# Second attention: the inverse softmax sums are spread over the heads' rows as a high and a low part, in two one-row-per-step passes

## The reference, cut to what matters

```python
Qp = query @ Wq + bq
K = _l2norm(key @ Wk + bk)
V = value @ Wv + bv
Q = _l2norm(Qp)
scores = jnp.einsum('bhqd,bhkd->bhqk', Q, K) * SCALE
attn = jax.nn.softmax(scores, axis=-1)
out = jnp.einsum('bhqk,bhkd->bhqd', attn, V)
...
out = out @ Wo + bo
x = out + Qp
mu = jnp.mean(x, axis=-1, keepdims=True)
var = jnp.mean((x - mu) ** 2, axis=-1, keepdims=True)
return (x - mu) / jnp.sqrt(var + LN_EPS) * ln_gamma + ln_beta
```

## Time and profile before

| | kernel before |
|---|---|
| median of three executions | 1012.98 us |
| the profiled execution | 1015.24 us |
| its span, first to last instruction | 1013.5 us |
| mean granted TensorE clock over the span | 0.948 of full speed |
| TensorE busy | 910.0 us (90%), 5517 matmuls |
| VectorE busy | 772.3 us (76%), 1837 instructions |
| ScalarE busy | 544.6 us (54%) |
| GpSimd busy | 351.3 us (35%) |
| the 42 float32 matmul instructions of the spreads in blocks 1 to 7 | first start 747.2, last start 930.2 us |

### The profile page before, as it was taken

The page is one execution under the profiler, slowest core; times in us unless marked ns, Lnnn a source line. Parts: engine busy times, 40 slices in busy tenths (PEclk is TensorE's granted clock), DMA queues, the critical chain, the costliest instruction groups (busy, mean ns, idle before and its releaser), DMA issues. The chain is left out here.

```text
span 1013.5 us, 17873 instructions
## 1 busy us (share of the span) xinstructions
PE 910.0 (90%) x5517; PEld 763.0 (75%) x5517; DVE 772.3 (76%) x1837; ACT 544.6 (54%) x1480; POOL 351.3 (35%) x409
## 2 busy tenths in 40 slices
PE   5899999999999969999899999946999999999535
PEld 4899999999999958888799999945655555555324
DVE  5698788788787567877677777757569888867977
ACT  4677567567566455444144444414465656554367
POOL 3134334334334236555600000067545465311320
PEclk9899999999999979999999999976999999999758
DMA  9999950000000023332133333351211011000003
GB/s 311 297 309 311 320 154 0 0 0 0 0 0 2 1 84 125 110 126 84 75 113 120 121 126 124 109 159 31 59 36 37 27 42 42 1 1 1 0 10 156
DMA packets 52616, 91.84 MB, mean 91 GB/s; under 512 B 5335, under 2 KB 27584, under 8 KB 52544
## 3 DMA queue, kind: packets, MB, share of 16 engines
q1 hardware_dynamic: 46400, 74.16, 23.7%
q0 software_dynamic: 6144, 16.79, 4.9%
HBM read 34.56 MB, written 56.36 MB: 90 GB/s over the span
## 5 line engine op out<-in xcount | busy, mean ns | idle before, releaser
L462 POOL TENSOR_TENSOR prob<-prob,row_inv 128x462 f32<-128x462 f32 (+1 forms) x96 | 83.8, 875 | 185.0 <-DVE row_inv L623 184.9
L794 PE MATMUL acc<-u,probT 128*128 128x256 f32 (+1 forms) x960 | 133.5, 289 | 0.9 <-DVE u L635 0.9
L522 ACT ACTIVATE prob<-score,neg_max 128x77 f32<-128x77 f32 x512 | 121.1, 350 | 13.3 <-DVE neg_max L617 13.0
L2287 POOL DMA_INDIRECT routed<-dispatched,slots x64 | 65.2, 1019 | 173.4 <-POOLq L1392 155.9
L748 PE MATMUL score<-m,xnT 128*128 128x462 f32 (+1 forms) x576 | 125.0, 355 | 0.0
L794 PEld LDWEIGHTS acc<-u,probT 128*128 128x128 f32 (+1 forms) x960 | 119.4, 189 | 1.9 <-DVE u L635 1.4
L748 PEld LDWEIGHTS score<-m,xnT 128*128 128x128 f32 x576 | 97.8, 191 | 6.3
L1098 PE MATMUL py<-w1T,hidT 128*128 x426 | 91.1, 349 | 0.4 <-DVE hidT L1316 0.4
L1367 POOL DMA_INDIRECT dispatched<-xn,slots x64 | 68.5, 1070 | 62.6 <-DVEq L1230 45.5
L512 ACT ACTIVATE probT<-tr 128x512 fp32r<-128x512 f32 (+1 forms) x96 | 51.7, 542 | 68.5 <-PE tr L734 68.1
L1843 PE MATMUL score<-qT,kbd 128*128 128x512 f32 (+1 forms) x240 | 79.4, 442 | 0.9 <-DVE qT L2068 0.7
(11 more groups left out here) (377 smaller groups left out, 2162.1 us busy)
## 6 DMA issues: line engine op xcount, KB each, us to landing
dispatched<-zeros SPq DMA_DIRECT2D x1, 33664.0 KB, 114.4
xn<-dispatched SPq DMA_DIRECT2D x71, 128.0 KB, 2.0
dispatched<-hid SPq DMA_DIRECT2D x71, 128.0 KB, 1.7
out<-x_res SPq DMA_DIRECT2D x8, 512.0 KB, 2.6
x_res<-in_x SPq DMA_DIRECT2D x1, 3072.0 KB, 15.2
consts<-in_L_ffn_W SPq DMA_DIRECT2D x8, 384.0 KB
consts<-in_L_ffn_Ws SPq DMA_DIRECT2D x3, 384.0 KB
x_res<-in_x SPq DMA_DIRECT2D x2, 512.0 KB, 9.3
```

Source lines behind the costliest of these rows:

```text
L462: gp.tensor_tensor(pr, pr, row_inv[t % 2][:, heads(k)].unsqueeze(2).to_broadcast([P, BANK_HEADS[k], KEYS]), ALU.mult).then_inc(prob_ready, 1)
L522: last = act.activation(prob[t % 2][:, h * KEYS:(h + 1) * KEYS], score_of(t, k)[:, n * KEYS:(n + 1) * KEYS], ACT.Exp, bias=neg_max[t % 2][ ...
L794: last = pe.matmul(acc[t % 2][:, 0:D], probT[t % 2][i][0:rows, c, :], u[k][0:rows, c, :], start=(c == 0 and q == 0), stop=(c == KCH - 1 an ...
L2287: gp.indirect_dma_start(out=routed[n % 2][:, k, j, :], out_offset=None, in_=xd, in_offset=bass.IndirectOffsetOnAxis(ap=g["slots"][:, n, k, ...
```

## The change

The spread is done on operands that a one-row-per-step pass can take. Once, during set-up, ScalarE rounds the 0/1 matrix into a new tile `spread_sums` of the one-pass type. In each block VectorE writes the reciprocals in place over `osum`, then copies them rounded into `oinv_hi`, then subtracts to have the rest in `oinv_lo`; each of the three steps raises `oinv_ready`, and each waits for the one before it. TensorE multiplies the high part and then the low part into the same bank. The same is done for the halves after block 7.

To make room, the last layer's small tiles now lie in the probability buffers `prob`, so that their filling moves: the bias load waits for the last value product, the two memsets move from ahead of block 0 to the end of GpSimd's list.

```diff
@@ attention1
-        oinv = sb("oinv", [P, TB], F32)
+        oinv_hi, oinv_lo = (sb(f"oinv_{n}", [P, TB], F32R) for n in ("hi", "lo"))
+        spread_sums = sb("spread_sums", [P, sum(SUM_ROWS)], F32R)
+        sum_spread = [spread_sums[:, sum(SUM_ROWS[:i]):sum(SUM_ROWS[:i + 1])] for i in range(DC + 1)]
...
-        ffn_bias, ident16 = sb("ffn_bias", [1, D], F32), sb("ffn_ident", [P, P], BF16)
+        ident16, ffn_bias = prob[0][:, 0:P // 2].bitcast(BF16), prob[2][0:1, 0:D]
...
@@ pe_spread (pe_spread_last alike)
-            pe.wait_ge(s["oinv_ready"], n + 1)
+            pe.wait_ge(s["oinv_ready"], 3 * (n + 1))
             if 3 * n + i:
                 pe.wait_ge(s["oT_ready"], 3 * n + i)
-            pe.matmul(wide[0:rows, :], g["spread_sum"][i][at, :], oinv[at, :], start=True, stop=True).then_inc(s["wide_mm"], 1)
+            pe.matmul(wide[0:rows, :], sum_spread[i][at, :], oinv_hi[at, :], start=True, stop=False)
+            pe.matmul(wide[0:rows, :], sum_spread[i][at, :], oinv_lo[at, :], start=False, stop=True).then_inc(s["wide_mm"], 1)
@@ ScalarE
+        def act_sum_spread(act):
+            act.activation(spread_sums[:, :], g["sum_spread"], ACT.Copy)
@@ VectorE
+        def dve_split_inverse(dve, m, at):
+            dve.wait_ge(s["oinv_ready"], 3 * m + 1)
+            dve.tensor_copy(oinv_hi[0:SUM_END, at], g["osum"][0:SUM_END, at]).then_inc(s["oinv_ready"], 1)
+            dve.wait_ge(s["oinv_ready"], 3 * m + 2)
+            dve.tensor_tensor(oinv_lo[0:SUM_END, at], g["osum"][0:SUM_END, at], f32(oinv_hi[0:SUM_END, at]), ALU.subtract).then_inc(s["oinv_ready"], 1)
+
         def dve_inverse_sums(dve, n):
             dve.wait_ge(s["sums_out"], 3 * (n + 1))
-            dve.reciprocal(oinv[0:SUM_END, :], g["osum"][0:SUM_END, :]).then_inc(s["oinv_ready"], 1)
+            dve.reciprocal(g["osum"][0:SUM_END, :], g["osum"][0:SUM_END, :]).then_inc(s["oinv_ready"], 1)
+            dve_split_inverse(dve, n, slice(0, TB))
@@ dve_inverse_sums_last: the same, with tokens(a) and dve_split_inverse(dve, LAST + a, tokens(a))
@@ SyncE
+                sp.wait_ge(s["pv_mm"], NC3 * (NBLK))
                 sp.dma_start(ffn_bias[:, :], w["L1_ffn_bias"].unsqueeze(0)).then_inc(fs["bias_in"], 16)
@@ GpSimd: from ahead of block 0 to behind gp_last_rstd_half(gp, 1)
+                gp.wait_ge(s["pv_mm"], NC3 * (NBLK))
                 gp.memset(bias_rows[:, :], 0.0).then_inc(fs["rows_set"], 1)
                 gp.memset(minus_one[:, :], -1.0).then_inc(fs["rows_set"], 1)
@@ ScalarE, set-up
-                for n in range(3):
+                for n in range(2):
                     act_weights(act, n)
+                act_sum_spread(act)
+                act_weights(act, 2)
```

More of the change, by code:

```diff
@@ L888, in attention1_constants @@
     at = [SUM_SPREAD_AT + sum(SUM_ROWS[:i]) for i in range(DC + 1)]
+    g["sum_spread"] = consts[:, SUM_SPREAD_AT:SUM_SPREAD_AT + sum(SUM_ROWS)]
     g["spread_sum"] = [consts[:, a:a + rows] for a, rows in zip(at, SUM_ROWS)]
@@ L1656, in attention1 @@
         SPREAD = [(b, c) for b in range(B) for c in range(C3)]
-        bias_rows, minus_one = sb("ffn_bias_rows", [BIAS_END, D], BF16), sb("ffn_minus_one", [BIAS_END, P], BF16)
-        ffn_bias, ident16 = sb("ffn_bias", [1, D], F32), sb("ffn_ident", [P, P], BF16)
+        ident16, ffn_bias = prob[0][:, 0:P // 2].bitcast(BF16), prob[2][0:1, 0:D]
+        minus_one, bias_rows = prob[1][0:BIAS_END, 0:P // 2].bitcast(BF16), prob[1][0:BIAS_END, P:P + D // 2].bitcast(BF16)
         amax, limit = sb("x_amax", [P, 1], F32), sb("x_limit", [1, 2], F32)
@@ L1826, in pe_spread_last @@
             at, rows = slice(SUM_AT[i], SUM_AT[i] + SUM_COLS[i]), SUM_ROWS[i]
-            pe.wait_ge(s["oinv_ready"], LAST + 1 + a)
+            pe.wait_ge(s["oinv_ready"], 3 * (LAST + 1 + a))
             if a == 0 and i == 0:
@@ L1831, in pe_spread_last @@
                 pe.wait_ge(s["acc_out"], 3 * LAST + i + 1)
-            pe.matmul(last_spread(i, a)[0:rows, tokens(a)], g["spread_sum"][i][at, :], oinv[at, tokens(a)], start=True, stop=True).then_inc(s["wide_mm"], 1)
+            bank = last_spread(i, a)[0:rows, tokens(a)]
+            pe.matmul(bank, sum_spread[i][at, :], oinv_hi[at, tokens(a)], start=True, stop=False)
+            pe.matmul(bank, sum_spread[i][at, :], oinv_lo[at, tokens(a)], start=False, stop=True).then_inc(s["wide_mm"], 1)
         def pe_scores(pe, n, c):
@@ L2110, in dve_inverse_sums_last @@
                 dve.wait_ge(s["sums_out"], 3 * (LAST + 1))
-            dve.reciprocal(oinv[0:SUM_END, tokens(a)], g["osum"][0:SUM_END, tokens(a)]).then_inc(s["oinv_ready"], 1)
+            dve.reciprocal(g["osum"][0:SUM_END, tokens(a)], g["osum"][0:SUM_END, tokens(a)]).then_inc(s["oinv_ready"], 1)
+            dve_split_inverse(dve, LAST + a, tokens(a))
         def dve_divide_last(dve, i, a):
@@ L2395, in _ @@
                 gp_gather(gp, 2, 2)
-                gp.memset(bias_rows[:, :], 0.0).then_inc(fs["rows_set"], 1)
-                gp.memset(minus_one[:, :], -1.0).then_inc(fs["rows_set"], 1)
                 for n in range(NBLK):
@@ L2406, in _ @@
                 step = lambda n: gp.wait_ge(fs["part_step"], n)
+                gp.wait_ge(s["pv_mm"], NC3 * (NBLK))
+                gp.memset(bias_rows[:, :], 0.0).then_inc(fs["rows_set"], 1)
+                gp.memset(minus_one[:, :], -1.0).then_inc(fs["rows_set"], 1)
                 gp.wait_ge(fs["bias_in"], 16)
```

## The result

| | kernel before | changed kernel |
|---|---|---|
| median | 1011.12 us (20 executions) | 1017.02 us (20 executions) |
| lowest | 1009.25 us | 1011.44 us |
| ratio to before, 95% interval | | 1.0049 [1.0037, 1.0061] |
| the profiled execution's span | 1013.5 us | 1015.6 us |

The time lies inside the range, but the sum said +0.8 us and "no change", and the measurement says +5.0 us (1.0049), more than the 0.3% that can be told from no change. The case with a chance of 0.20 came. One of the changed kernel's twenty executions took 1803.52 us at a granted clock of 1.00; it is left out of the ratio, and without it the median is 1016.92.

The account below looks back on a forecast made before the run. TensorE looked like the bound, VectorE close behind. Blocks 2 to 5 +1.32, block 1 -0.10, block 6 -0.06, block 7 -1.18, afterwards +0.80: +0.78 on 1012.98 gave 1013.8 us, range 1009.0 to 1017.5.

Parts of the forecast that it names:

- The case with a chance of 0.20: Whole kernel: slower than before by over 0.3%, chance 0.20.
- What bounds the kernel: Inner blocks: TensorE looks like the bound, with VectorE arriving nearly together at the `proj` hand-over and the second transposes.
- TensorE's gain: Spreads on TensorE: two passes take 0.59 us instead of 1.02, saving 0.43 a spread, 1.28 a block.
- VectorE's cost: Between reciprocals and `qp`: a cast of 0.43 and a subtraction of 0.69 bring `qp` 1.18 us later.
- The dear ends: Rival: copy at 0.69 us gives 1015.9, with bare second weight loads too 1017.0; chance 0.14.
- Blocks 2 to 5: Each block loses 1.08 us at the hand-over and wins 0.75: +0.33 each, +1.32 in all.
- 0.10 of slack: Hand-over of `proj`, blocks 2 to 6: 0.1 us of slack cuts the 1.18 us delay to 1.08.
- blocks 1 and 6: Block 1: 1.18 lost, 1.28 won, -0.10 us; block 6: 1.08 lost, 1.14 won, -0.06 us.
- Block 7: No query projection there: first spread 0.10 us late, the 1.28 of the spreads won, -1.18 us.
- The clock: Rival: new standstills of 1.08 and 0.53 us lower the clock in blocks 1 to 6, giving 1024 us; chance 0.08.
- After block 7: Casts and subtractions for both halves add 1.5 us ahead of the first division; the last division ends +0.80 us later.
- At nothing: Set-up copy, moved memsets and bias load lie in idle time or far ahead of use: 0 us.

Follow-up runs that it names:

- e2: Changed kernel with TensorE's part only: no cast or subtraction, both passes multiply the rounded reciprocals; timed -8.9 us against the kernel before.
- e3: Changed kernel with VectorE's part only: cast and subtraction stay, spreads are float32 products of the unsplit reciprocals; timed +8.5 us against the kernel before.
- e11: e4 with float32 spreads after block 7, last-norm statistics moved between the query splits, their aggregation behind the second; timed -0.7 us against the kernel before.
- e14: Kernel before with only the last-norm statistics moved between the query splits and their aggregation behind the second; timed +3.3 us against the kernel before.
- e7: e3 with one useless subtraction of 256 columns added in block 7 between cast and subtraction; timed +11.8 us against the kernel before.
- e1: Changed kernel with the small step `shift_f` moved ahead of the reciprocals on VectorE; timed +4.3 us against the kernel before.
- e4: Changed kernel with VectorE's order reciprocals, `shift_f`, first `qp`, then cast and subtraction; ratio 0.9979 to the kernel before.

## Why the prediction was right or wrong

**What bounds the kernel: right.** TensorE and VectorE arrive nearly together at the hand-over of `proj` and at the second transposes. e2 and e3 move an inner block by -0.83 and +1.25 us, so both are on the path. That ScalarE, and the path to `y`, would come next (e11, e14) the prediction did not say; nothing in its sum hangs on it.

**TensorE's gain: right, a little large.** A pair takes 0.64 us and not 0.59, so a spread saves 0.38, not 0.43. The second load lies under the first product (920.86 and 920.94 are the starts of two loads of 0.15 and 0.16 us, the products start 0.31 apart), so the rule of the Trainium skill ("TensorE: Matmul & The Clock Gate", Part 3, section "The mechanism"), by which it would be bare, does not show here (the same section also lets a load into the background weight buffer go ahead, which no run here can tell apart).

**VectorE's cost: right.** 0.42 and 0.69 against 0.43 and 0.69; `qp` 1.18 later as worked out. The slope behind it was part luck: it set a subtraction of 512 columns beside a copy of 256 out of PSUM (0.415), and the subtraction of 256 columns then took 0.42 as well. The dear ends of that rival did not come.

**Blocks 2 to 5: the mechanism was right, the size too small**, +0.42 each and not +0.33. I took 0.10 of slack off the stall and so let all that follows be 1.08 late. But the slack was TensorE's. VectorE runs nearly without a break from the reciprocals to its first division (0.14 us of idle time before), so its own list passes on the full 1.18, and a little more (+1.25 in e3). The other side, 0.75 won, measured 0.83 in e2. In blocks 1 and 6 the same 0.1 to 0.2 is missing.

**Block 7: the step that failed.** It said "with 1.18 and a signal it is 0.10 late, and the rest is won", -1.18, and it looked only at the spread, the one consumer of what was split. But what stands behind an inserted step on its engine is delayed as well, and `shift_f` stood there. Its path over ScalarE's norm, the exponentials and the score bank had 0.3 us of slack in the kernel before (exponentials at 923.34, scores at 924.37, where after they follow within 0.72), and the split took 1.2. The wait gave the gain back (parts: +0.86 and -0.86), and the lower clock put 1.7 to 3.4 us on top. With `shift_f` ahead of the split the block wins 0.89, three quarters of what I had said.

**The clock: a rival, in the wrong place.** "The clock within a block falls" was one of my signs of being wrong, and it came. I asked whether the stall at the hand-over, 1.08 us in blocks 1 to 6, would lower the clock. It did not in the changed kernel, at 1.16 us in blocks 2 to 6 and 1.74 in block 1. It fell in block 7, behind a wait of 1.07 that I had not seen. So the price that I gave for one gap, 1.7 us, was paid once or twice over, but not six times.

**After block 7: right in kind, +1.15 and not +0.80.** The splits end 4.96 us behind the start of the reciprocals, as worked out within 0.15. Then I had the divisions wait for spreads and end 3.0 us later; VectorE needs 3.2 for them one after another, without a wait.

**At nothing** stood the moved memsets, bias load and set-up copy: behind `y` the changed kernel is at 0.00 and +0.35 in its two profiled executions, and nothing waits for them.

**The range held** by luck. Its upper end of 1017.5 was there for a dear copy and bare loads, and neither came; the lower clock, which did, had been left out of it. And the kernel before took 1011.12 beside the changed one; on the 1012.98 from which I had worked, the measured ratio gives 1017.9. The chance of 0.67 for no change was too high: blocks 2 to 5 and the last stretch alone, where the costs had been worked out nearly to size, came to +2.8 us, and only the -1.18 of block 7 brought the sum back to nothing.

## What to carry to other kernels

Work that is put into an engine's list is paid by everything behind it, down to its smallest step. List for each of these who waits for it and with how much slack, before counting what the new result's own consumer gains. Where a stall grows on TensorE, price it at both clock levels. And halves of a change that trade one engine for another are worth running apart: here their sum gave six of seven blocks to a few hundredths, and the seventh, where it did not, pointed at the clock.

## What the runs showed of the hardware

The length of a wait does not tell by itself whether the granted clock falls. In blocks 2 to 6 of the changed kernel TensorE stands still for 1.13 to 1.17 us in each and the clock stays at 1.00. In block 7 a wait of 1.07 (three of three profiled executions) or of 0.31 and 0.68 close together (e7, one execution) is followed by some 3.4 or 6.8 us at the lower level, and one of 0.67 (e3, one execution) is not. In block 1 the same wait of 1.74 or 1.75 us stands in seven executions; the clock stays at 1.00 in six and falls in one (e7), on the same code as e3. A wait of 2.49 in block 4 of e1 is followed by some 3.4 us at the lower level. The windows ahead of the waits in blocks 4 and 7 of the changed kernel both show TensorE busy throughout; what tells them apart stays open. The low stretch itself varies between executions of one kernel, 3.4 us lost in one and 1.7 in the other. So of a single execution neither a fall nor its absence is proof; that `shift_f` behind the split brings it in block 7 rests on three executions with it and six without.

The end of the last layer, some 50 us behind an edit of 1.15 us, took 1.9 us more in four kernels of four, with the lower level there (0.50 to 0.53 in the window of 5 us that begins 50 us behind `y`, 1.00 there in e4 and the changed kernel). Its cause was not tried.
